# Dense experts' first steps in a two-layer decoder kernel: the order of one silu, and the way of the first pairs' shares

## The reference

```python
x = h.reshape(Bb * Tt, Hh)                     # 1,024 tokens x 256, after a layer norm
logits = x @ gate_w.T                          # 64 experts
topv, topi = jax.lax.top_k(logits, TOP_K)      # 8 of them
rw = jax.nn.softmax(topv)
W = zeros((N, E)).at[arange(N)[:, None], topi].set(rw)      # the shares
gu = jnp.einsum('nh,eih->nei', x, gu_w)        # every expert for every token
gate, up = gu[..., :I], gu[..., I:]            # I = 64
inter_w = jax.nn.silu(gate) * up * W[:, :, None]
out = jnp.einsum('nei,ehi->nh', inter_w, dp_w)
out = out + sigmoid(x @ sh_gate1_w.T) * shared_expert(x)
```

## Time and profile before

| | us |
|---|---|
| median of three executions (936.4 to 938.04) | 937.77 |
| the profiled execution's own time | 932.93 |
| its span, first to last instruction | 931.2 |

### The profile page before, as it was taken

How to read it: one execution, slowest core, us unless ns; L and a number is a source line. 1 busy time by engine, 2 the same in 40 slices (tenths; PEclk the granted TensorE clock), 3 DMA queues, 4 the chain that set the end, 5 groups by cost and what they waited for, 6 DMA issues and landing times.

```text
span 931.2 us, 16611 instructions
## 1 busy us (share of the span) xinstructions
PE 800.3 (86%) x5619; PEld 531.3 (57%) x5626; DVE 656.9 (71%) x1388; ACT 552.3 (59%) x1735; POOL 304.3 (33%) x266
## 2 busy tenths in 40 slices
PE   3898887549999178957999999999779999999997
PEld 2677665417877147724677777778434444444443
DVE  2775587848985389639999999896535555566664
ACT  1778766236776157736878777776334444444442
POOL 1111245740000577117545555541012222222220
PEclk9999999569999589989999999999989999999999
DMA  9970001126995221010000000002234444444421
GB/s 299 401 301 2 2 13 47 69 89 233 321 337 207 76 71 56 1 54 1 1 2 1 1 2 1 1 2 75 78 83 121 119 117 118 117 117 116 121 84 46
DMA packets 35888, 90.82 MB, mean 98 GB/s; under 512 B 6502, under 2 KB 9065, under 8 KB 35306
## 3 DMA queue, kind: packets, MB, share of 16 engines
q1 hardware_dynamic: 32746, 81.63, 26.8%
q0 software_dynamic: 3072, 8.30, 2.8%
HBM read 67.71 MB, written 22.29 MB: 97 GB/s over the span
## 4 chain that ended last, share of the span: by engine, by line
PE 46%; DVE 6%; ACT 2%; issue 1%; POOL 1%; DMA 1%; DVEq 0%; SPq 0%; ACTq 0%
PE xpr L1532 9%; PE xps L1532 9%; PE xpr L1430 7%; PE xpt L1547 5%; PE xpo L1547 4%; PE xpo L1477 4%; PE xps L1445 2%; PE xpo L1467 2%; PE xpt L1487 1%; PE xpt L1453 1%; DVE xqr L1737 1%; POOL xsr L1109 1%; DVE xt L1723 1%; DVE xqr L1720 1%; DVE xmx L1742 0%
## 5 line engine op out<-in xcount | busy, mean ns | idle before, releaser
L1124 POOL TENSOR_TENSOR m1ws<-rows,m1ws 128x768 f16<-128x768 f32 x33 | 54.1, 1641 | 202.9 <-ACT rows L1386 171.9
L1264 ACT ACTIVATE xsq<-xt 128x512 f16<-128x512 f32 x66 | 41.5, 629 | 111.3 <-DVE xt L1823 111.3
L1532 PE MATMUL xps<-red,m1ws 128*128 128x512 f16 x396 | 92.4, 384 | 2.6 <-DVE xt L1823 2.6
L1532 PE MATMUL xpr<-red,m1ws 128*128 128x512 f16 x396 | 91.9, 382 | 1.4 <-DVE xt L1823 1.4
L1104 POOL TENSOR_TENSOR xqr<-xqr,xt 128x512 f32<-128x512 f32 x48 | 66.2, 1380 | 53.1 <-DVE xt L1723 52.7
L1827 DVE TENSOR_TENSOR xsq<-xt,xsq 128x512 f16<-128x512 f32 x66 | 45.6, 691 | 41.9 <-ACT xsq L1264 41.7
L1962 POOL DMA_INDIRECT rows<-slots_out,slot x32 | 33.5, 1047 | 113.2 <-DMA slots_out<-m0yo 101.4
L1532 PEld LDWEIGHTS xps<-red,m1ws 128*128 128x128 f16 x396 | 39.1, 99 | 50.4 <-issue 5.1
L1532 PEld LDWEIGHTS xpr<-red,m1ws 128*128 128x128 f16 x396 | 39.0, 99 | 48.7 <-issue 3.5
L1201 ACT ACTIVATE xsq<-xpr 128x128 f32<-128x128 f32 x192 | 50.6, 284 | 15.8 <-PE xpr L1430 15.6
L1547 PE MATMUL xpt<-xsq,m1ws 128*128 128x512 f16 x198 | 49.4, 387 | 6.3 <-DVE xsq L1827 6.3
(11 more groups left out here) (301 smaller groups left out, 2034.4 us busy)
## 6 DMA issues: line engine op xcount, KB each, us to landing
rows<-in_m_w SPq DMA_DIRECT2D x33, 384.0 KB, 4.0
slots_in<-m0h SPq DMA_DIRECT2D x1, 8192.0 KB, 26.5
m0rg<-in_m_wgu SPq DMA_DIRECT2D x16, 512.0 KB, 5.4
m0xg<-slots_in SPq DMA_DIRECT2D x32, 256.0 KB, 3.8
slots_out<-m0yo SPq DMA_DIRECT2D x32, 256.0 KB, 3.1
ang<-wt_dram SPq DMA_DIRECT2D x20, 256.0 KB, 3.8
turns<-wt_dram SPq DMA_DIRECT2D x20, 256.0 KB, 3.9
red<-wt_dram SPq DMA_DIRECT2D x20, 256.0 KB, 3.8
```

The source lines that it names most:

```text
L1124: pool.tensor_tensor(ws[:, u, 1, :], raw[:, u, :], ws[:, u, 0, :], ALU.subtract).then_inc(prep_ok, 1)
L1532: ins = pe.matmul(bank, part(u, sw, c, which), hx[:, sh, c, CH * q:CH * q + CH], start=(i == 0), stop=(i == 5))
```

## The change

Two edits. On ACT, the silu of job 5 and the `act_high` of job 4 are issued ahead of `prep_high(3)`, the split of the fourth pair. On SP, the shares of the first three pairs go straight from `WT[q]` in SBUF to the 64 partitions each; the source of each transfer is one row in one partition, read 64 times. The store to DRAM is issued behind these six transfers, and SP waits for it only once, ahead of the loads for pairs 3, 4 and 5.

```diff
             for q in range(NCH):
                 cols = slice(CH * q, CH * q + CH)
                 copied(sp, "W", q)
+                for p in range(NR):
+                    for h in range(2):
+                        row = WT[q][2 * p + h:2 * p + h + 1, :]
+                        sp.dma_start(Wb[p][64 * h:64 * h + 64, cols], row.unsqueeze(1).to_broadcast([1, 64, CH])).then_inc(b_in[p] if q else b_first[p], 16)
                 sp.dma_start(wt_dram[:, cols], WT[q]).then_inc(stored, 16)
-                sp.wait_ge(stored, 16 * q + 16)
-                for p in range(NR):
-                    load_b(p, p, cols, b_in[p] if q else b_first[p])
                 if q == 0:
                     for p in range(NR):
                         sp.wait_ge(prep_ok, p + 1)
                         load_raw(p + NR, p)
+            sp.wait_ge(stored, 16 * NCH)
             for p in range(NR):
                 sp.wait_ge(sw_ok, NR + p + 1)
                 load_b(p + NR, p, slice(0, B * S), b_in[p])
```

```diff
             silu(3, 1)
             silu(4, 0)
             act_high(3, 1)
-            prep_high(3)
             silu(5, 1)
             act_high(4, 0)
+            prep_high(3)
             act_high(5, 1)
             prep_high(4)
             silu(6, 0)
```

## The result

The changed kernel took 952.57 us (median of four executions, 947.89 to 957.55) beside 937.90 us for the kernel before in the same series: a ratio of 1.0161, with a 95% interval of 1.0131 to 1.0190. A second series of both gave 950.90 beside 939.45, 1.0121 (1.0091 to 1.0152). The prediction was 949, slower.

A forecast was written before the change was run, and what follows sets the result against it. It took the waits ahead of `hidden(6)`, the loop's first step, as the bound. Slow SBUF transfers cost 11 us: 932.93 + 11 = 944, with the median 4.8 above, so 949; range 928 to 956, slow case 942 to 955.

The forecast's parts named there:

- The service of one partition: Shares' transfers: one SBUF row read 64 times takes 4.84 us, 27 GB/s; slow service was given 0.61.
- The sum: Slow case: six transfers a chunk at 4.84 us make `hidden(6)` start 4.5 to 17.4 us later.
- The low end: Third pair's two transfers run beside the first four; `hidden(6)` starts 4.5 us later, median 942.
- the high end: All six transfers in one line, 29 us, behind chunk 0's backlog; 17.4 us later, median 955.
- The middle: Between low and high end: 11 us later, 944 for an execution like the profiled one, 949 for the median.
- The silu's move: `silu(5)` ahead of pair 3's split on ACT: by itself, `hidden(6)` starts earlier, 4.6 to 5.6 us gained.
- One sentence on it: Sign to look for on ACT: pair 3's split starts right after `down(3)`, with `silu(5)` ahead of it, in any case.
- Six of about half a microsecond: SP's issues of a chunk's six share transfers stay at about half a microsecond each.
- the backlog that the sum's high end had: Chunk 0's transfers, then the store and three raw loads, 1.3 MB, 3 us; chunk 1 gets data from 671.
- The clock: PE idles ahead of `down(4)`, so in the slow case it takes 2.74 us again, where the loop's takes 1.29.

The follow-up runs named there:

- chunk 1 alone: Changed kernel, but only chunk 1's shares go straight from SBUF, chunk 0's by way of DRAM: 950.91 us beside 937.78 before, ratio 1.0136.
- The pair of runs with four partitions: Changed kernel, but each transfer reads four partitions 16 times: neighbours 0 to 3 took 959.07 us, partitions 0, 4, 8 and 12 took 932.89.
- the run with chunk 0 alone: Changed kernel, but only chunk 0's shares go straight from SBUF, chunk 1's by way of DRAM: 937.32 us beside 937.78 before, ratio 0.9996.
- the best version: Changed kernel, but each transfer reads eight copies of its row, written by one more DVE instruction: 931.93 us beside 939.45 before, ratio 0.9917.
- the silu alone: Kernel before with only the silu's move, shares still by way of DRAM: 931.09 us beside 937.78 before, ratio 0.9939.

## Why the prediction was right

**The service of one partition.** The sum took 4.84 us for a transfer, 27 GB/s. The window shows 27 GB/s, and with chunk 1 alone six transfers take 28.8 us. The sum left open whether one DMA engine or a group of partitions sets that rate. The pair of runs with four partitions showed it: neighbours share one way out.

**How far the transfers overlap.** The low end let the third pair run wholly beside the first two, the high end not at all. Counted from the first issue, the low end had pairs 0 and 2 there after 10.9 and 20.6 us, the high end after 15.4 and 34.8; measured were 12.9 and 27.9. The middle, 11 us later, met the 11.8 of the stretch, but by a choice between ends and not by a working that told where between them: that part was luck. With 27.9 put in, the sum gives 10.4 us. The other 1.4 are the later turn of chunk 1's shares, 29.0 us after that of chunk 0 in place of 27.6, because job 0 waits for its shares; the sum had no such term.

**The silu's move.** Its 4.6 to 5.6 us were right for itself, and it is worth nothing behind late shares. One sentence on it was wrong: the split should have started right after `down(3)` in any case. ACT's timeline in the changed kernel (`silu(5)`, `act_high(4)`, the split):

```profile
691.84 0.60 ACT L1260 ACTIVATE xqr<-xps 128x512 f32<-128x512 f32 x1 [2.24 <-PE xps L1534]
696.94 0.63 ACT L1266 ACTIVATE xsq<-xt 128x512 f16<-128x512 f32 x1 [4.51 <-DVE xt L1825]
697.48 0.83 ACT L1255 ACTIVATE m1ws<-rows 128x768 f16<-128x768 f32 x1
```

`act_high(4)`, brought ahead of the split, waits for `times_up(4)`, which waits for late shares; the split stands behind it. It cost nothing here, since `down(4)` was later still.

**The issues.** "Six of about half a microsecond" was wrong: SP stood for 18.5 us in chunk 1's six issues (674.65 to 693.12). That was not on the path for chunk 1, but in chunk 0 it held up the raw loads behind it. Where a store stands next, as in the run with chunk 0 alone, that costs 3.7 us. In the changed kernel no such store is waited for, and the backlog that the sum's high end had (3 us of transfers behind chunk 0's) hardly shows: pair 0 of chunk 1 is there 12.9 us after the first issue, against 11.7 with chunk 1 alone, and pair 2 after 27.9, against 28.8.

**The clock.** `down(4)` was taken at 2.74 and measured at 2.74; the granted clock in the wait ahead of it is 0.50. The longer waits also slowed `hidden(4)`, which the sum did not have; it lay beside the wait for pair 0 and cost nothing.

## What to carry to other kernels

Before a broadcast is moved from DRAM to SBUF, ask how many partitions its source has and whether they are neighbours: by way of DRAM the first pair's shares were there 5.7 us after the issue of the store, far cheaper than six reads of 4.8 us each out of neighbouring partitions. Look for the second use of a queue: transfers that merely take longer hold up the issuing engine, and everything that is issued behind them. And in a list written out by hand, first ask which call stands behind a wait that it doesn't need; moving one silu ahead of a split gave 0.6%, most of what the best version gained.

## What the runs showed of the hardware

- All 16 DMA engines read one SBUF partition at 27 GB/s together, while one DRAM row, read the same way, landed in 3.1 us a transfer. Four neighbouring partitions gave 28 GB/s, four that lie four apart 99, at the same share of busy engines.
- The engine that issues a transfer can stand at the issue for as long as a transfer takes: the last two of a chunk took 9.45 us to issue, the first two 1.11.
- Transfers from different groups of partitions on one queue overlap in part: 54 GB/s where one group gives 27.
- Whether PE's clock falls is not told by the length of one wait. The granted clock in `hidden(5)` was 0.61 behind a wait of 2.56 us in the profiled execution of before, and 1.00 behind 2.39 with the silu alone; in `hidden(4)` of the changed kernel it was 0.50 behind 2.18.
